# A cross-attention and spectral feed-forward kernel: Query fills ahead of the value products up to slot 12, GpSimd's long additions behind VectorE's zero test

## The chip, the cores and the metric

The kernel runs on one core of a Trainium2 chip. The metric is the device time of one execution in microseconds (us), the median of several runs. An execution is also recorded by the hardware profiler; its rows are what this document reads. Engines: PE is TensorE (PEld its weight loads), DVE is VectorE, ACT is ScalarE, POOL is GpSimd, SP is the queue that issues most DMAs.

## The reference

```python
x = x + xattn(layernorm(x), ctx, mask)      # 2 x 2048 tokens, 512 channels, 16 heads of 32, 128 keys
x = x + ffn(layernorm(x))

def xattn(z, ctx, mask):
    q, k, v = z @ wq + bq, ctx @ wk + bk, ctx @ wv + bv
    score = (q k^T / sqrt(32)) * mask
    score = where(score == 0, -1e9, score)
    return softmax(score) v @ wo + bo

def ffn(z):
    return real(ifft(fft(z) @ w_freq)) + bias
```

The feed-forward part is linear, so the kernel builds one real 512 x 512 matrix for it (fills U and M below) and multiplies by that.

## The kernel before, in words

The 4096 tokens are cut into 16 chunks of 256 (index `c`), the 16 heads into 4 groups of 4 (index `g`). One pair (chunk, group) is a step `s = 4c + g`; there are 64 steps. All engines run the same loop over slots `v` from 2 to 79, with `c, r = divmod(v, 4)`; each engine has its own fixed order inside a slot, and semaphores join them. There is no scheduler beyond `plan()` and the order in which each engine's code is written.

In slot v TensorE does, in this order (`plan()`, `items`):

1. PT(v-2): eight transposes of the exponentials of step v-2 (L540).
2. the slot's "mid" fills: WO (output projection, in slots with r = 0, 1), FF (feed-forward, r = 2, 3), and early in the program V, U and M.
3. S(v+1): the scores of the next step (L528).
4. PV(v-3): two transposes of the reciprocal sums (L553) and the products of step v-3 with the values (L557).
5. the slot's "late" fills: Query projections Q(c, f), twelve matmuls (L485) and one for the bias row (L488). Slots 2, 4 and 6 have two of them, the others one; from slot 55 there are none.

Fills go round three PSUM banks: `fill()` waits until VectorE has freed the bank of the fill three places before (`g_free`). In a slot with one mid fill a Query fill so waits for the mid fill of the slot before. Where fills come closer (the second Query fills of slots 4 and 6, the Query fills of slots 5, 7, 8 and 9, and the M fill of slot 11) the fill three places before is the Query fill before it.

ScalarE in slot v: `copy_rec(v-4)` (L655, waits for PV(v-4)), half of the exponentials of step v-1 (L642, wait for `nbias`), `copy_pt(v-2)` (L651, waits for PT(v-2)), the other half, `ctx_hi(v-4)` (L662, `ch`), in slots 9 to 12 `high_m` (L621, `mh`), then the high halves `qh` of the Query fills of the slot before (L616) and the `od` of U and M fills.

VectorE in slot v: `mask_mul(v)` (L799), `zero_to_neg(v)` (L806, the zero test: it writes `(z == 0) - z` over z), `ctx_norm(v-4)` (L822, `cn`), `least(v)` (L811), in slots 9 to 12 `low_m` (`ml`), then the low halves of the fills (L772 `ql`, which free the Query banks; L778, L784 for WO and FF), statistics, the reciprocal `rz` of step v-2 (L816), in slots 4 and 5 three additions `fold` (L854).

GpSimd in slot v: `spread(v-3)` (L1034, `rzb`, which PV(v-3) waits for), small statistics, `bias(v)` (L1028, `nbias`), subtractions for the feed-forward (L1003 `x1nl`), `add_bf`, `ctx_lo(v-4)` (L1039, `cl`, which WO waits for), `add_bo` (L990, adds the output bias to the input rows), `scale_mask` (L1021), `split_lo` (L983, `xtl`), and in slot 3 `low_o` (the low half `wol` of the output weights).

Of the kernel before, what the change touches and what calls it, by code (L numbers as in the profile page):

```python
# [5 lines left out]
ALU = mybir.AluOpType  # L6
# [6 lines left out]
D = 512  # L13
# [4 lines left out]
NC = NB * S // CH  # L18
NS = 4 * NC
V0, V1 = 2, NS + 16  # L20
LAST = ("FF", NC - 1, 1)
NEG = 1e9
MASK_SCALE = 1e-9 / 32.0 ** 0.5 / 8.0
# [2 lines left out]
NX = 7  # L26
NM = 4
NT = 2
# [6 lines left out]
def plan():  # L35

    fills, slots, held = [], {}, []
    lead = [("W1", 0), ("CT", 0), ("CT", 1), ("K", 0), ("ST", 0), ("Q", 0, 0), ("Q", 0, 1), ("S", 0),
            ("W1", 1), ("Q", 0, 2), ("S", 1), ("K", 1), ("Q", 0, 3), ("ST", 1), ("Q", 1, 0), ("S", 2),
            ("Q", 1, 1), ("Q", 1, 2), ("Q", 1, 3)]
    front = []
    for f in lead:
        if f[0] == "S":
            front += [("S", f[1], 0), ("S", f[1], 1)]
        else:
            front.append(("G", len(fills)))  # L50
            fills.append(f)
    early = {
        2: [("V", 0), ("ST", 2)], 3: [("V", 1)],
        4: [("U", 0)], 5: [("U", 1)], 6: [("U", 2)], 7: [("U", 3)],
        8: [("M", 0)], 9: [("M", 1)], 10: [("M", 2)], 11: [("M", 3)],
    }
    queries = {2: [(2, 0), (2, 1)], 3: [(2, 2)], 4: [(2, 3), (3, 0)], 5: [(3, 1)], 6: [(3, 2), (3, 3)]}
    for v in range(V0, V1):
        c, r = divmod(v, 4)
        mid = {  # L60
            0: [("WO", c - 2, 0)],
            1: [("WO", c - 2, 1)],
            2: [("FF", c - 3, 0)],
            3: [("FF", c - 3, 1)],
        }[r]
        mid = [f for f in mid if 0 <= f[1] < NC] + early.get(v, [])
        if mid == [LAST]:
            mid = [LAST, (*LAST, "right")]
        late = [("Q",) + f for f in queries.get(v, [divmod(v + 9, 4)]) if f[0] < NC]
        base = len(fills)  # L70
        fills += mid + late
        mids = list(range(base, base + len(mid)))
        lates = list(range(base + len(mid), len(fills)))
        items = []
        if 0 <= v - 2 < NS:
            items += [("PT", v - 2, 0), ("PT", v - 2, 1)]
        items += [("G", n) for n in mids]
        if 0 <= v + 1 < NS:
            items += [("S", v + 1, 0), ("S", v + 1, 1)]
        if 0 <= v - 3 < NS:  # L80
            items += [("PV", v - 3)]
        items += [("G", n) for n in lates]
        slots[v] = (items, held, mids)
        held = lates
    return fills, front, slots
# [6 lines left out]
def small_slot(c):  # L92
    return 2 if c == 3 else 4 * (c - 3)
# [4 lines left out]


def lo_slot(c):  # L100
    return 3 if c == 3 else 4 * (c - 3) + 2


def bo_slot(c):
    return c + 5 if c < 5 else 4 * (c - 3) + 3


def build(nc, x, xt, ctx_in, mask, wq, bq, wk, bk, wv, bv, wo, bo, lparts, tables, bf, eye, sums, pick, out):
# [3 lines left out]
    with ExitStack() as stack:  # L112
        def sem(name):
            return stack.enter_context(nc.semaphore(name))
# [6 lines left out]
        def sb(name, shape, dt, where=None):  # L121

            n = 2 if dt == F16 else 4
            for s in shape[1:]:
                n *= s
            n = (n + 31) // 32 * 32
            a = pos[0] if where is None else where
            if where is None:
                pos[0] += n
            assert a + n <= top, (name, a + n, top)  # L130
            return nc.alloc_sbuf_tensor_at(name, shape, dt, offset=a), a

        xs, _ = sb("xs", [128, NX, 2, D], F32)
        xtr, _ = sb("xtr", [128, NT, 4, CH], F32)
        xth, a_xth = sb("xth", [128, 2, 4, CH], F16)
        xtl, a_xtl = sb("xtl", [128, 2, 4, CH], F16)
# [35 lines left out]
        bob, _ = sb("bob", [128, D], F32)  # L172
# [41 lines left out]
        PB, CX, G = bank[0:2], bank[2], bank[3:6]  # L214
# [21 lines left out]
        g_free, tt_done, eq_done, mn_done = (sem(n) for n in ("g_free", "tt_done", "eq_done", "mn_done"))  # L236
# [5 lines left out]
        p_l1, p_l2, p_zero = (sem(n) for n in ("p_l1", "p_l2", "p_zero"))  # L242
        p_const, p_ms, p_nb, p_cl, p_st, p_xb, p_r2, p_x1b, p_sm, l_done, p_rz = (
            sem(n) for n in ("p_const", "p_ms", "p_nb", "p_cl", "p_st", "p_xb", "p_r2", "p_x1b", "p_sm", "l_done", "p_rz"))
# [6 lines left out]
        def tile_of(c, t):  # L251
            return 2 * c + t

        def columns(n):

            if fills[n] == LAST:
                return slice(0, 256)
            return slice(256, 512) if fills[n][:3] == LAST else slice(0, 512)

# [698 lines left out]
        def _(pool):  # L958
            small = [0]

            def step(ins):
                small[0] += 1
                ins.then_inc(p_sm, 1)
                pool.wait_ge(p_sm, small[0])
# [13 lines left out]
                step(pool.tensor_copy(z, h16[:].unsqueeze(2).broadcast_to([128, 2, 2, 2])))  # L978
                pool.tensor_tensor(stok[:, c % 2, :, 2:4], a, h16[:], ALU.subtract).then_inc(p_st, 1)

            def split_lo(c):
                pool.wait_ge(h1_done, c + 1)
                pool.tensor_tensor(xtl[:, c % 2], xtr[:, c % NT], xth[:, c % 2], ALU.subtract).then_inc(p_l1, 1)  # L983

            def add_bo(c, t):
                if c == 0 and t == 0:
                    pool.wait_ge(d_bb, 2 * 16)
                pool.wait_ge(a1_done, 2 * c + t + 1)
                z = xs[:, c % NX, t, :]
                pool.tensor_tensor(z, z, bob[:], ALU.add).then_inc(p_xb, 1)  # L990

            def rstd2(c, t):
                n = tile_of(c, t)
                pool.wait_ge(a2_done, n + 1)
                step(pool.tensor_scalar(ve2[:, t:t + 1], ag2[:, t, 1:2], EPS, SO * SO, ALU.add, ALU.mult))
                if n >= NO:
                    pool.wait_ge(g_free, at["FF", (n - NO) // 2, t] + 1)
                pool.tensor_tensor(rs2[:, n % NO:n % NO + 1], ve2[:, t:t + 1], half[:, 0, 0:1], ALU.pow).then_inc(p_r2, 1)
# [6 lines left out]
            def add_bf(c, t):  # L1005
                n = tile_of(c, t)
                pool.wait_ge(s2_done, n + 1)
                if c == NC - 1:
                    pool.wait_ge(l2_done, t + 1)
                else:  # L1010
                    pool.wait_ge(p_l2, n + 1)
                pool.wait_ge(p_r2, n + 1)
                z = x1[:, n % NO, :]
                pool.tensor_tensor(z, z, bfb[:], ALU.add).then_inc(p_x1b, 1)
# [15 lines left out]
            def spread(s):  # L1030
                pool.wait_ge(rz_done, s + 1)
                if s >= 2:
                    pool.wait_ge(pv_done, s - 1)
                pool.tensor_copy(rzb[:, s % 2], rz[:, s % 4, :].unsqueeze(2).broadcast_to([128, 8, 32])).then_inc(p_rz, 1)  # L1034
# [30 lines left out]
            def low_o():  # L1065
                pool.wait_ge(w_hi, 3)
                for i in range(2):
                    k = slice(2 * i, 2 * i + 2)
                    pool.tensor_tensor(wol[:, k], wos[:, k], woh[:, k], ALU.subtract).then_inc(o_lo, 1)
# [38 lines left out]
            for v in range(V0, V1):  # L1108
                c, r = divmod(v, 4)
                if v == 8:  # L1110
                    constant_row()
                if 0 <= v - 3 < NS:
                    spread(v - 3)
                for a in range(5, NC):
                    if small_slot(a) == v:
                        stat_cols(a)
                if r == 1 and 0 <= c - 2 < NC:
                    rstd2(c - 2, 0)
                if r == 2 and 0 <= c - 2 < NC:
                    rstd2(c - 2, 1)  # L1120
                if 0 <= v < NS:
                    bias(v)
                if r == 2 and 0 <= c - 2 < NC - 1:
                    norm_lo2(c - 2, 0)
                if r == 3 and 0 <= c - 2 < NC - 1:
                    norm_lo2(c - 2, 1)
                if r < 2 and 0 <= c - 3 < NC:
                    add_bf(c - 3, r)
                if 0 <= v - 4 < NS:
                    ctx_lo(v - 4)  # L1130
                for a in (3, 4):
                    if small_slot(a) == v:
                        stat_cols(a)
                for a in range(NC):
                    if bo_slot(a) == v:
                        add_bo(a, 0)
                    if bo_slot(a) + (2 if a >= 5 else 0) == v:
                        add_bo(a, 1)
                if r == 0 and 2 <= c + 1 < NC:
                    scale_mask(c + 1)  # L1140
                for a in range(3, NC):
                    if lo_slot(a) == v:
                        split_lo(a)
                if v == 3:
                    low_o()


def frequencies():
# [82 lines left out]
```

## Time and profile before

| | |
|---|---|
| median of 3 runs | 466.74 us (466.25 to 467.75) |
| profiled execution | 467.02 us |
| its span | 465.2 us |
| TensorE busy | 446.9 us, 96% |
| VectorE busy | 410.0 us, 88% |
| ScalarE busy | 375.9 us, 81% |
| GpSimd busy | 372.6 us, 80% |
| granted TensorE clock | 1.00 of full speed |

The span is the time between the first and the last recorded instruction; the profiled execution's own time is 1.8 us longer. A busy share is an average over the whole program: the start (to slot 12, about 120 us), the steady part and the end behave differently, and must be read apart. The first lines below name instructions by line of the kernel before.

### The profile page before, as it was taken

The numbers are of one execution on the slowest core, as the hardware profiler recorded it, in microseconds if no ns is written. First come the engines' busy times: TensorE is split into PE (matmuls) and PEld (weight loads), VectorE is DVE, ScalarE is ACT, GpSimd is POOL, SyncE is SP. The second block draws the span as 40 slices with busy tenths as digits, with TensorE's granted clock in tenths as the row PEclk, the third lists the DMA queues.
The fourth block names the chain that finished last, engine by engine and source line by source line (L and its number), as shares of the span: only waits on it lengthen the run. The fifth ranks groups of instructions, "written<-read, shape, count | busy, mean of one in ns | idle before, by whom it ended". The sixth has DMA issues, their size and how long they took to land.

```text
span 465.2 us, 11189 instructions
## 1 busy us (share of the span) xinstructions
PE 446.9 (96%) x3550; PEld 297.2 (64%) x3550; DVE 410.0 (88%) x627; ACT 375.9 (81%) x1432; POOL 372.6 (80%) x520
## 2 busy tenths in 40 slices
PE   7989977999999999999999999999999999999897
PEld 6777656676566666666666666666666666655444
DVE  3797499889999999999999999999999998999443
ACT  3359766789998989899989898998989898989720
POOL 6589666995989989898989898998989784876663
PEclk9999999999999999999999999999999999999999
DMA  8996644122435454545445454445342323340244
GB/s 290 394 360 171 235 173 113 45 82 70 104 76 138 115 138 105 141 120 132 131 116 134 104 130 117 107 108 144 103 103 57 99 75 77 82 92 20 73 103 124
DMA packets 83452, 59.36 MB, mean 128 GB/s; under 512 B 39746, under 2 KB 70978, under 8 KB 82883
## 3 DMA queue, kind: packets, MB, share of 16 engines
q1 hardware_dynamic: 82960, 58.55, 45.2%
q8 instruction: 29, 0.48, 0.4%
q14 instruction: 29, 0.23, 0.2%
q10 hardware_dynamic: 434, 0.10, 0.1%
HBM read 29.27 MB, written 8.39 MB: 81 GB/s over the span
## 4 chain that ended last, share of the span: by engine, by line
PE 79%; DVE 8%; issue 5%; POOL 4%; SPq 2%; DMA 1%; ACT 0%; POOLq 0%; DVEq 0%
PE bank L410 32%; PE bank L485 16%; PE bank L540 10%; PE bank L557 7%; PE scores L528 5%; PE bank L415 3%; PE bank L553 3%; DVE zs L799 2%; SPq L269 2%; PE bank L563 2%; DMA xs<-in_x 1%; DVE nmin L811 1%; PE bank L488 1%; DVE zs L806 1%; POOL cl L1039 1%
## 5 line engine op out<-in xcount | busy, mean ns | idle before, releaser
L642 ACT ACTIVATE zs<-zs,nbias 128x128 f32<-128x128 f32 x512 | 199.6, 397 | 6.4 <-POOL nbias L1028 6.2
L642 ACT ACTIVATION_READ_ACCUMULATOR zs<-zs,nbias 128x1 f32 x512 | 99.3, 194 | 0.0
L806 DVE SCALAR_TENSOR_TENSOR zs<-zs 128x1024 f32<-128x1024 f32 x64 | 94.8, 1481 | 2.2
L799 DVE TENSOR_TENSOR zs<-scores,ms 128x1024 f32<-128x1024 f32 x64 | 77.9, 1218 | 0.0
L811 DVE TENSOR_REDUCE nmin<-zs 128x8 f32<-128x1024 f32 x64 | 77.1, 1205 | 0.1
L651 ACT COPY pt<-bank 128x512 f32<-128x512 f32 x128 | 68.3, 586 | 7.0 <-PE bank L540 5.0
L485 PE MATMUL bank<-xth,wqh 128*128 128x256 f16 x256 | 70.3, 275 | 2.0 <-DVE kl L758 2.0
L485 PE MATMUL bank<-xtl,wqh 128*128 128x256 f16 x256 | 69.8, 273 | 0.0
L485 PE MATMUL bank<-xth,wql 128*128 128x256 f16 x256 | 69.8, 273 | 0.0
L540 PE MATMUL bank<-ident,zs 128*128 128x128 f32 x512 | 67.0, 274 | 0.5 <-ACT zs L642 0.5
L1034 POOL COPY rzb<-rz 128x256 f32<-128x256 f32 x64 | 61.0, 953 | 3.1 <-DVE rz L816 2.2
L540 PEld LDWEIGHTS bank<-ident,zs 128*128 128x128 f32 x512 | 56.8, 140 | 5.3 <-ACT zs L642 3.6
L1028 POOL TENSOR_SCALAR nbias<-nmin 128x8 f32<-128x8 f32 x64 | 15.7, 246 | 50.2 <-DVE nmin L811 50.2
L410 PE MATMUL bank<-woh,ch 128*128 128x512 f16 x128 | 48.5, 379 | 1.8 <-POOL cl L1039 1.8
L410 PE MATMUL bank<-woh,cl 128*128 128x512 f16 x128 | 48.5, 379 | 0.0
L410 PE MATMUL bank<-wol,ch 128*128 128x512 f16 x128 | 48.5, 379 | 0.0
L655 ACT COPY rec<-bank 128x256 f32<-128x256 f32 x64 | 23.9, 373 | 29.4 <-PE bank L557 29.0
L410 PE MATMUL bank<-mh,x1h 128*128 128x512 f16 x120 | 45.5, 379 | 0.0
L410 PE MATMUL bank<-mh,x1l 128*128 128x512 f16 x120 | 45.5, 379 | 0.0
L410 PE MATMUL bank<-ml,x1h 128*128 128x512 f16 x120 | 45.5, 379 | 0.0
L1039 POOL TENSOR_TENSOR cl<-cn,ch 128x256 f16<-128x256 f32 x64 | 43.5, 680 | 1.7 <-ACT ch L662 1.7
L528 PEld LDWEIGHTS scores<-ks,qs 96*128 96x128 f16 x480 | 31.8, 98 | 15.4 <-DVE zs L799 2.0
(109 smaller groups left out, 973.8 us busy)
## 6 DMA issues: line engine op xcount, KB each, us to landing
xs<-in_x SPq DMA_DIRECT2D x16, 512.0 KB, 4.2
xtr<-in_xt SPq DMA_DIRECT2D x16, 512.0 KB, 4.8
out<-x SPq DMA_DIRECT2D x31, 256.0 KB, 2.5
qs<-qh SPq DMA_DIRECT2D x120, 64.0 KB, 2.0
lp<-in_lparts SPq DMA_DIRECT2D x4, 1024.0 KB, 9.1
qs<-ql SPq DMA_DIRECT2D x60, 64.0 KB, 2.0
ms<-in_mask SPq DMA_DIRECT2D x16, 128.0 KB, 2.4
wqs<-in_wq SPq DMA_DIRECT2D x2, 512.0 KB, 6.7
```

What stands on the lines that cost most here:

```text
L410: last = pe.matmul(o, a, b, start=(i == 0), stop=(i == len(mm) - 1))
L485: pe.matmul(o[:, 0:256], a, b, start=(i == 0), stop=False)
L528: last = pe.matmul(A[:, n % 2, 128 * j:128 * j + 128], qs[c % 2][0:96, g, j, 128 * t:128 * t + 128], ks[0:96, g, j, c // (NC // NB), :], s ...
L540: last = pe.transpose(PB[f][:, a:a + 128], zs[:, s % NZ, t, 2 * f + i, :], ident[:])
L557: last = pe.matmul(CX[32 * j:32 * j + 32, 0:256], vs[:, b, h:h + 32], pt[:, s % 2, j, :], start=True, stop=True)
L642: last = act.activation(z, z, ACT.Exp, bias=nbias[:, s % 4, i:i + 1], scale=-NEG, accum_out=zsum[:, s % 4, i:i + 1])
L651: act.copy(pt[:, s % 2, 2 * f:2 * f + 2, :], PB[f][:]).then_inc(pt_copied, 1)
L799: dve.tensor_tensor(zs[:, s % NZ], A[:].rearrange("p t (h k) -> p t h k", h=4), ms[:, c % NM].unsqueeze(2).broadcast_to([128, 2, 4, KEYS]) ...
L806: dve.scalar_tensor_tensor(out=z, in0=z, scalar=0.0, in1=z, op0=ALU.is_equal, op1=ALU.subtract).then_inc(eq_done, 1)
L811: dve.tensor_reduce(nmin[:, s % 4, :], zs[:, s % NZ].rearrange("p t h k -> p (t h) k"), AX.X, ALU.min).then_inc(mn_done, 1)
L1034: pool.tensor_copy(rzb[:, s % 2], rz[:, s % 4, :].unsqueeze(2).broadcast_to([128, 8, 32])).then_inc(p_rz, 1)
L1039: pool.tensor_tensor(cl[:, c % 2, g, :], cn[:, s % 2, :], ch[:, c % 2, g, :], ALU.subtract).then_inc(p_cl, 1)
```

## The change

Three things are changed.

`plan()`: in slots up to 12 the late fills stand before PV(v-3). From slot 13 the order is as it was.

GpSimd, place and size of the two-tensor operations: `add_bo(a, 0)` and `split_lo(a)`, the latter cut into two halves in two slots, stand before `bias(v)` from slot 9 on, behind a new wait for `eq_done` (VectorE's zero test of this slot). `add_bo(a, 1)` is cut into halves three slots apart. The bias additions of chunks 0 to 2 go from slots 5, 6, 7 to slots 7, 8, 9, those of chunks 3 and 4 from 8, 9 to 11, 15 and those of later chunks from slot 4a-9 to 4a-1.

GpSimd, other moves: `spread(v-2)` at the end of slot v instead of `spread(v-3)` at the start, from slot 4 on; so it is ahead of `scale_mask` and `split_lo`. `low_o` in slot 3 goes ahead of `split_lo(3)`.

```diff
-        if 0 <= v - 3 < NS:
-            items += [("PV", v - 3)]
-        items += [("G", n) for n in lates]
+        weigh = [("PV", v - 3)] if 0 <= v - 3 < NS else []
+        queue = [("G", n) for n in lates]
+        items += queue + weigh if v <= 12 else weigh + queue
...
 def bo_slot(c):
-    return c + 5 if c < 5 else 4 * (c - 3) + 3
+    return c + 7 if c < 3 else 4 * c - 1
...
-                if 0 <= v - 3 < NS:
+                if v <= VP and 0 <= v - 3 < NS:      # VP = 4
                     spread(v - 3)
...
+                if VS <= v < NS:                     # VS = 9
+                    pool.wait_ge(eq_done, v + 1)
+                for a in range(5, NC):
+                    if v == 4 * a - 11:
+                        split_lo(a, slice(0, 2), False)
+                    if v == 4 * a - 10:
+                        split_lo(a, slice(2, 4))
+                for a in range(3, NC):
+                    if bo_slot(a) == v:
+                        add_bo(a, 0)
                 if 0 <= v < NS:
                     bias(v)
...
+                if v == 3:
+                    low_o()
                 if 0 <= v - 4 < NS:
                     ctx_lo(v - 4)
...
+                for a in range(3, NC):
+                    if bo_slot(a) == v:
+                        add_bo(a, 1, slice(0, D // 2), False)
+                    if bo_slot(a) + 3 == v:
+                        add_bo(a, 1, slice(D // 2, D))
+                for a in (3, 4):
+                    if lo_slot(a) == v:
+                        split_lo(a)
+                if v >= VP and 0 <= v - 2 < NS:
+                    spread(v - 2)
```

TensorE in slot 7, before: S(8), then PV(4), then Q(4, 0), then the first rows of slot 8 (the lines of the changed kernel are numbered three higher: 531 is 528, 488 is 485, 556 is 553).

```order
L528 MATMUL scores<-ks,qs_63 128x128 [waits d_q0,tt_done]
L528 MATMUL scores<-ks,qs_63 128x128 x3
L553 MATMUL bank<-ident,rzb 128x128 [waits p_rz,cn_done,pt_copied]
L553 MATMUL bank<-ident,rzb 128x128
L557 MATMUL bank<-pt,vs 32x256 x4
L485 MATMUL bank<-xth,wqh 128x256 [waits p_l1,w_lo,g_free]
L488 MATMUL bank<-srow,wz 128x256 [waits st_done,wz_lo]
L540 MATMUL bank<-ident,zs 128x128 [waits pt_copied,ex_done]
```

The same place in the changed kernel.

```order
L531 MATMUL scores<-ks,qs_63 128x128 [waits d_q0,tt_done]
L531 MATMUL scores<-ks,qs_63 128x128 x3
L488 MATMUL bank<-xth,wqh 128x256 [waits p_l1,w_lo,g_free]
L491 MATMUL bank<-srow,wz 128x256 [waits st_done,wz_lo]
L556 MATMUL bank<-ident,rzb 128x128 [waits p_rz,cn_done,pt_copied]
L556 MATMUL bank<-ident,rzb 128x128
L560 MATMUL bank<-pt,vs 32x256 x4
L543 MATMUL bank<-ident,zs 128x128 [waits pt_copied,ex_done]
```

The Query fill with its wait for a free bank now stands ahead of the products; of its thirteen matmuls the first and the last are shown, and of the scores the first half.

GpSimd in slots 4 and 5, before: `scale_mask(2)`, then slot 5 with `spread(2)`, `bias(5)`, `ctx_lo(1)`, both additions `add_bo(0)`, and `spread(3)`, which is slot 6's.

```order
L1021 TENSOR_SCALAR ms<-ms,rs_95 128x128 [waits p_st,d_m2]
L1021 TENSOR_SCALAR ms<-ms,rs_95 128x128
L1034 COPY rzb<-rz 128x256 [waits pv_done,rz_done]
L1028 TENSOR_SCALAR nbias<-nmin 128x8 [waits ex_done,mn_done]
L1039 TENSOR_TENSOR cl<-cn,ch 128x256 [waits ch_done]
L990 TENSOR_TENSOR xs<-xs,bob 128x512 [waits a1_done,d_bb]
L990 TENSOR_TENSOR xs<-xs,bob 128x512 [waits a1_done]
L1034 COPY rzb<-rz 128x256 [waits pv_done,rz_done]
```

The same stretch in the changed kernel.

```order
L1041 COPY rzb<-rz 128x256 [waits pv_done,rz_done]
L1028 TENSOR_SCALAR ms<-ms,rs_95 128x128 [waits p_st,d_m2]
L1028 TENSOR_SCALAR ms<-ms,rs_95 128x128
L1035 TENSOR_SCALAR nbias<-nmin 128x8 [waits ex_done,mn_done]
L1046 TENSOR_TENSOR cl<-cn,ch 128x256 [waits ch_done]
L1041 COPY rzb<-rz 128x256 [waits pv_done,rz_done]
```

`spread(2)` has gone ahead of the mask scaling, and the two additions have left slot 5.

GpSimd in slots 10 and 11 of the changed kernel: half of `split_lo(5)` and the addition `add_bo(3, 0)` stand ahead of the `nbias` of their slot, the first of them in a slot with the wait for `eq_done`.

```order
L986 TENSOR_TENSOR xtl<-xtr,xth 128x512 [waits h1_done,eq_done]
L1035 TENSOR_SCALAR nbias<-nmin 128x8 [waits ex_done,mn_done]
L1010 TENSOR_TENSOR x1nl<-x_76,x1nh 128x512 [waits h2_done]
L1046 TENSOR_TENSOR cl<-cn,ch 128x256 [waits ch_done]
L1041 COPY rzb<-rz 128x256 [waits pv_done,rz_done]
L995 TENSOR_TENSOR xs<-xs,bob 128x512 [waits a1_done,eq_done]
```

Before, both stood at the end of a slot, behind `ctx_lo`, and `split_lo` was one instruction of 1024 columns.

## Rows read from the trace of the kernel before

**Rows 1.** Busy time by stretch: start:end us, length, PE, PEld, DVE, ACT, POOL, clock, DMA.
```profile
57.60:117.00 59.40, 51.13 (x423) 38.76 (x422) 55.38 (x92) 46.96 (x183) 43.98 (x60) 1.00 0.33 97
120.00:390.00 270.00, 270.00 (x2228) 177.46 (x2229) 259.57 (x385) 244.08 (x948) 238.72 (x331) 1.00 0.44 113
390.00:436.00 46.00, 43.86 (x335) 24.84 (x334) 41.37 (x60) 43.87 (x184) 30.86 (x46) 1.00 0.31 72
```

**Rows 2.** Chain of waits, steady part: start us, us, what.
```profile
245.41 0.45 PE scores L528 x8
245.86 0.23 PE bank L553 x2
246.08 0.57 PE bank L557 x8
246.65 1.42 PE bank L485 x12
248.07 0.11 PE bank L488
...
251.64 0.45 PE scores L528 x8
```

**Rows 3.** Timeline of TensorE, start: start us, us, instruction [idle before <-releaser].
```profile
60.77 0.41 PE L553 MATMUL bank<-ident,rzb 128*128 128x128 f32 x2 [1.27 <-DVE cn L822]
...
69.22 0.41 PE L553 MATMUL bank<-ident,rzb 128*128 128x128 f32 x2 [1.47 <-POOL rzb L1034]
...
74.71 1.97 PE L415 MATMUL bank<-tb,lp 128*128 128x256 f32 x8 [2.11 <-issue]
...
85.45 0.41 PE L553 MATMUL bank<-ident,rzb 128*128 128x128 f32 x2 [0.93 <-POOL rzb L1034]
...
103.82 1.04 PE L540 MATMUL bank<-ident,zs 128*128 128x128 f32 x8
...
113.65 0.41 PE L553 MATMUL bank<-ident,rzb 128*128 128x128 f32 x2 [1.02 <-issue]
...
117.26 0.38 PE L410 MATMUL bank<-woh,ch 128*128 128x512 f16 x1 [0.24 <-POOL cl L1039]
```

**Rows 4.** Timeline of ScalarE in slots 8 and 9.
```profile
86.50 0.37 ACT L655 COPY rec<-bank 128x256 f32<-128x256 f32 x1 [0.58 <-PE bank L557]
...
91.23 0.37 ACT L616 CAST qh<-bank 128x256 f16<-128x256 f32 x1
...
99.19 0.63 ACT L621 ACTIVATE mh<-mf 128x512 f16<-128x512 f32 x1
```

**Rows 5.** Timeline of VectorE, slots 4 to 11.
```profile
57.60 1.22 DVE L799 TENSOR_TENSOR zs<-scores,ms 128x1024 f32<-128x1024 f32 x1
...
61.72 0.41 DVE L772 TENSOR_TENSOR ql<-bank,qh 128x256 f16<-128x256 f32 x1
...
63.52 1.99 DVE L854 TENSOR_TENSOR lp<-lp 128x512 f32<-128x512 f32 x3
...
70.74 3.87 DVE L854 TENSOR_TENSOR lp<-lp 128x512 f32<-128x512 f32 x3
...
91.66 0.41 DVE L772 TENSOR_TENSOR ql<-bank,qh 128x256 f16<-128x256 f32 x1
...
110.73 1.23 DVE L799 TENSOR_TENSOR zs<-scores,ms 128x1024 f32<-128x1024 f32 x1
```

**Rows 6.** Timeline of GpSimd, slots 5 and 6.
```profile
68.67 0.40 POOL L1034 COPY rzb<-rz 128x256 f32<-128x256 f32 x1
...
70.31 2.95 POOL L990 TENSOR_TENSOR xs<-xs,bob 128x512 f32<-128x512 f32 x2
...
81.84 3.13 POOL L983 TENSOR_TENSOR xtl<-xtr,xth 128x1024 f16<-128x1024 f32 x1
```

**Rows 7.** VectorE's zero test and least, all 64 each: ns min/median/max, first and last start.
```profile
L806 DVE SCALAR_TENSOR_TENSOR zs<-zs x64: 1224/1403/2486, 23.4 to 427.8; 128x1024 f32<-128x1024 f32 x64
```
```profile
L811 DVE TENSOR_REDUCE nmin<-zs x64: 1201/1203/1220, 25.0 to 429.4; 128x8 f32<-128x1024 f32 x64
```

## What I expect of the change

> **What bounds the kernel now.** I read the busy table by stretch first, then the chain of waits, then the timelines of the start. From 120 to 390 us TensorE is busy 270 of 270 us [rows 1], and the chain runs on TensorE alone: one slot takes 251.64 - 245.41 = 6.23 us, score to score [rows 2]. In it the Query fill costs 1.42 + 0.11 = 1.53 us, the products 0.23 + 0.57 = 0.80. Nothing that other engines gain there shortens the kernel. From 390 to 436 TensorE is busy 43.9 of 46 us and VectorE 41.4 [rows 1]; there are no Query fills left there. In the start, 57.6 to 117 us, TensorE has 59.4 - 51.1 = 8.3 us of idle time, VectorE 4.0 [rows 1]. The seven rows of its timeline show where: products that wait 1.27, 1.47, 0.93 and 1.02 us, a U fill that waits 2.11, a WO fill 0.24 [rows 3]. Only there can this change be worth anything: the order change ends at slot 12, and after it the program is TensorE's work, so a shift at slot 13 goes unchanged to the end.
>
> **GpSimd's moves, from slot 13 on.** They shorten VectorE's zero test, 1403 ns in the median and 1224 at least, up to 2486 [rows 7]. The gain per slot is 0.2 to 0.3 us of an engine that is busy 259.6 of 270 us but doesn't set the end: 0 us. The Trainium skill (SBUF — State Buffer, "SBUF: two separate sides") says that a VectorE instruction with two SBUF inputs and a GpSimd one that reads SBUF exclude each other for a whole instruction. The trace fits only in part: the 1024-column subtraction at 81.84 took 3.13 us beside a zero test. By that rule all 64 zero tests would fall to the least of them and VectorE would lose 64 x (1.48 - 1.22) = 16 us of work, and a kernel that VectorE bounds would gain as much; TensorE's full rows say that this one isn't.
> The new wait holds `nbias` and all behind it back. `least` takes 1.20 us in every one of 64 cases [rows 7], `cn` comes before it, so there are about 1.5 us for an addition of some 1.3 (I take half of the two in 2.95 less what the folds cost them, [rows 6]) or a half split of about 1.1. Cost 0; if it isn't covered, ScalarE's exponentials start late by up to 0.3 us once in four slots, which a slot's slack on ScalarE (270 - 244 over 43 slots, 0.6 us) takes in. In the end part nothing long is moved into VectorE's way: 0.
>
> **GpSimd's moves in the start.** The two additions that ran at 70.31 for 2.95 us leave slot 5. Beside them VectorE's three folds took 3.87 us, without them 1.99 [rows 5, 6]: VectorE gains 1.9 us just where the U fill waits 2.11 us for the folds [rows 3]. `spread(2)`, done at 68.67 behind the mask scaling, comes 1.7 us earlier, but see below. `low_o` before `split_lo(3)` takes about 0.2 us off the zero test of slot 4. On SP the load of chunk 5's transposed input waits for `split_lo(3)`, about 1 us later than before: it isn't needed for several slots. The DMAs that stack the Query of chunk 2 wait for the same `ql` as before, 0.2 us later: free.
>
> **The order change.** A Query fill ahead of the products fills the products' wait, but ScalarE's slot starts with a copy of the products' result. So the products 1.53 us later are ScalarE's whole slot 1.53 us later. That matters where the next Query fill waits for the bank of the one before: slots 4 to 9. The loop there is then: Query fill 1.53, products 0.80, to ScalarE 0.07 (85.45 + 0.41 + 0.57 against 86.50), from `rec` to `qh` 91.23 - 86.50 = 4.73, to `ql` 0.43, `ql` 0.41, back to TensorE 0.06: 8.03 us [rows 2 to 5]. Before, the products were not in this loop, and the copy with the first exponentials ran beside the Query fill. I walk through it, from slot 4, whose start at 57.60 hangs on a DMA and stays.
> - Slot 4: the second Query fill needs the `ql` of 61.72 + 0.41 [rows 5], now about 61.9. It runs 61.95 to 63.5, the products to 64.3. Before they ended at 60.77 + 0.98 = 61.75.
> - Slot 5: 64.3 + 0.07 + 4.73 + 0.43 + 0.41 + 0.06 = 70.0 for the Query fill; before it followed the products at 69.22 + 0.98 = 70.2. Gain 0.2; the filled wait of 1.47 us is worth no more, since the fill waits for its bank. Products end 72.3, before 70.2.
> - Slot 6: VectorE starts at 73.0 instead of 74.5 (1.9 less 0.4 of waiting for `qh`), the U fill at 73.2 instead of 74.7. But the second Query fill waits for the loop: 70.0 + 8.0 = 78.0. Products end 80.3. So the 1.5 us are given back.
> - Slot 7: loop 8.03 and one more ScalarE copy of about 0.26 (an estimate from its neighbours of the same size): 86.3. Before, 85.45 + 0.98 = 86.4. Even, but the products still have to come: transposes of slot 8 start 86.3 + 1.53 + 0.80 = 88.6, before 86.43 + 1.53 = 87.96: 0.7 late.
> - Slot 8: loop 94.3, TensorE's own work gives the same. Still 0.7.
> - Slot 9: loop with `mh` (0.53 on ScalarE, [rows 4]) and `ml` ahead of `ql`, about 0.3 net: 94.3 + 8.9 = 103.2. With products and the statistics row the transposes of slot 10 start at 105.6, before 103.9 [rows 3]: 1.7 late.
> - Slots 10 and 11: ScalarE has its copy at 105.7, `mh` ends 105.7 + 4.75 + 0.63 = 111.1; VectorE then has 2.4 us of `ml`, `ql`, M and statistics, so its slot 11 starts at 113.5 instead of 110.73 [rows 5]: 2.8 late. The products' wait at 113.65 (1.02) is covered, but the scores of step 12 now wait for VectorE, to 114.8.
> - Slot 12: WO waits for GpSimd's `cl`, which comes behind VectorE's slot 11: 113.5 + 3.9 for `nbias`, then 0.2 + 1.16 + 0.67 and the hand-over: 119.5, before 117.26 [rows 3]. With its 0.1 us of start-up saved: 2.1 late.
> - Slot 13: the products again come first and wait 0.5 us for a `cn` that is late: 2.6.
> Sum: 467.02 + 2.6 = 469.6 for an execution like the profiled one, which is 0.28 above the median: 469.3 us. Each of the five loops may be off by 0.15 us and the ends of slots 10 to 13 by 1: 468.1 to 471.0.
>
> **Rivals.** (A) Faster. ScalarE takes the later copy in (in slot 6 it idled before `ch`) and the fills wait for VectorE as before. Then the folds' 1.9 us and about 0.6 us of shorter zero tests stay, 2.5 us in all, and the products' waits no longer matter: 467.0 - 2.5 = 464.5, 464.2 against the median. For it: VectorE is busy 55.4 of 59.4 us in this stretch. Against it: the loop of 8.0 us is made of rows, and slots 5 to 7 already take 8 us each (69.22, 77.4, 85.45). It decides if `qh` comes in time for `ql` in slots 5 to 9. The skill's port rule is no more than a part of this case.
> (B) No change. The 0.7 us of slot 7 are kept, but slots 9 to 12 catch up because `mh` finds room: 467.4. For it: in slots 8 and 9 the loop and TensorE's work are equal to 0.1 us, so small errors decide whether lateness grows.
> (C) Slower still: in slots with r = 1 GpSimd reaches `nbias` late already, the half split adds 1.1 us before it, ScalarE's slack is not enough, and 0.3 us are lost in each of 13 chunks: 3.9 more, 473.2.
>
> **How the numbers follow.** The forecast has 0.60, A 0.18, B 0.17, C 0.05. A measurement can tell about 0.3%, 1.4 us, from no change: faster is under 465.3, slower over 468.1. B is within; of the forecast's 0.60 I count 0.04 as within. So faster 0.18, same 0.21, slower 0.61. The likeliest case's own range is 468.1 to 471.0. The range that is to hold 8 in 10 takes in B and the upper edge of A and leaves C out: 464.9 to 471.2.
>
> **What would show it.** Right: in slots 5 to 9 the Query fill waits for `ql` (1 to 3 us before it in slots 5 and 7), the products never wait, ScalarE's `rec` in slot 7 starts near 80.4 with no transposes to wait for; transposes of slot 8 near 88.6; WO of slot 12 near 119.5; slots after 13 still 6.23 us, zero tests from slot 9 on near 1.25 us. The three folds of slot 5 in 2.0 us. Wrong: if VectorE has no wait for `qh` in slots 6 to 8, it is A. If the steady slots are not 6.23 us, the argument that only the start counts falls.

## The result, and the profile after

| | before | changed kernel |
|---|---|---|
| median | 466.81 us (466.25 to 467.75, 4 runs) | 473.52 us (472.73 to 474.73, 4 runs) |
| profiled execution | 467.02 us | 474.20 us |
| span | 465.2 us | 472.4 us |
| granted clock, mean | 1.00 | 0.993 |

The ratio is 1.0139 (95% interval 1.0118 to 1.016): slower by 6.5 us (6.7 by the two medians), where 2.6 us were forecast. The direction was right, the time lies above the stated range of 464.9 to 471.2 us, and above the likeliest case's own, 468.1 to 471.0. It lies near the 473.2 us of rival C, but nothing of C's mechanism is seen below: that is chance.

Busy time of the changed kernel by the same stretches as [rows 1] (start:end us, length, PE, PEld, DVE, ACT, POOL, clock, DMA):

```profile
57.60:117.00 59.40, 50.87 (x385) 37.31 (x383) 47.23 (x81) 41.94 (x166) 34.05 (x53) 0.94 0.29 87
120.00:390.00 270.00, 268.46 (x2211) 175.92 (x2204) 248.41 (x391) 243.74 (x950) 232.77 (x353) 1.00 0.44 112
```

In the start TensorE has as much busy time as before for fewer matmuls (385 records against 423), and VectorE has 8 us less of it for fewer instructions (81 against 92): both get through less work in the same time. And the granted clock is 0.94 there, where it was 1.00.

The steady part is as it was, 250.85 - 244.62 = 6.23 us from score to score as in [rows 2], in the changed kernel's chain of waits:

```profile
244.62 0.45 PE scores L531 x8
...
250.85 0.45 PE scores L531 x8
```

The place where the time goes is TensorE's timeline of the start, which answers to [rows 3] (start us, us, instruction [idle before <-releaser]):

```profile
61.80 0.28 PE L488 MATMUL bank<-xth,wqh 128*128 128x256 f16 x1 [1.01 <-DVE ql L775]
...
69.74 0.28 PE L488 MATMUL bank<-xth,wqh 128*128 128x256 f16 x1 [2.36 <-DVE ql L775]
...
70.08 0.27 PE L488 MATMUL bank<-xth,wqh 128*128 128x256 f16 x1
...
71.14 0.42 PE L488 MATMUL bank<-xth,wqh 128*128 128x256 f16 x1
...
79.20 0.28 PE L488 MATMUL bank<-xth,wqh 128*128 128x256 f16 x1 [0.78 <-DVE ql L775]
...
87.41 0.40 PE L488 MATMUL bank<-xth,wqh 128*128 128x256 f16 x1 [2.63 <-DVE ql L775]
...
105.84 0.28 PE L488 MATMUL bank<-xth,wqh 128*128 128x256 f16 x1 [0.69 <-DVE ql L775]
...
117.44 0.62 PE L531 MATMUL scores<-ks,qs 96*128 96x128 f16 x8 [0.64 <-DVE zs L802]
...
122.83 0.38 PE L413 MATMUL bank<-woh,ch 128*128 128x512 f16 x1 [1.54 <-POOL cl L1046]
```

Up to slot 12 no products wait any more; five Query fills wait for `ql`, 7.5 us in all. And within the fill that starts at 69.74 the same matmul goes from 0.27 to 0.42 us: the clock has fallen. In the fill at 87.41 the first matmul already takes 0.40. The windows say so (start:end us, length, PE busy, granted clock, DMA):

```profile
66.00:69.00 3.00, 1.38 (x13) 1.00 0.00 0
69.00:72.00 3.00, 2.26 (x14) 0.72 0.18 43
72.00:75.00 3.00, 3.00 (x22) 0.71 0.41 97
...
84.00:87.00 3.00, 0.78 (x10) 1.00 0.00 0
87.00:90.00 3.00, 2.59 (x13) 0.56 0.18 44
```

Twice TensorE stands still for 2.4 and 2.6 us, and twice the clock drops from its upper level (2.4 GHz) to the lower one (1.2 GHz) for some 3.5 us behind that. Query fill and products, 2.33 us at full clock, took 73.69 - 69.74 = 3.95 and 91.36 - 87.41 = 3.95 us (both ends from the chain of waits): 1.6 us more, twice.

ScalarE in slot 7 shows the loop (timeline; the copy `rec` waits for the products, and all else follows it):

```profile
81.64 0.37 ACT L658 COPY rec<-bank 128x256 f32<-128x256 f32 x1 [2.69 <-PE bank L560]
...
83.47 1.05 ACT L654 COPY pt<-bank 128x512 f32<-128x512 f32 x2
...
86.25 0.37 ACT L587 CAST srow<-bank 64x256 f16<-64x256 f32 x1
86.52 0.64 ACT L619 CAST qh<-bank 128x256 f16<-128x256 f32 x2
```

VectorE waits 2.43 us for that `qh`, and TensorE at 87.41 for its `ql`.

What GpSimd's moves were to do, they do. The three folds of slot 5 take 2.17 us instead of 3.87, and the zero test 1225 ns in the median instead of 1403:

```profile
70.71 2.17 DVE L857 TENSOR_TENSOR lp<-lp 128x512 f32<-128x512 f32 x3
```
```profile
L809 DVE SCALAR_TENSOR_TENSOR zs<-zs x64: 1224/1225/1869, 23.5 to 434.9; 128x1024 f32<-128x1024 f32 x64
```

To follow the loss I compare the start of VectorE's `mask_mul(v)` in both traces, slot by slot: -0.1 us in slot 4, -1.7 in 6, +0.4 in 7, +1.5 in 8, +3.8 in 9, +4.7 in 10, +5.4 in 11, +5.6 in 12 and 13. From slot 43 to 60 it stays at +5.4 to +5.5. In slot 61 it jumps to +7.1, and so it ends. So two places: 5.5 us up to slot 13, 1.6 us in slot 60. The second I had not foreseen at all. GpSimd in slots 58 to 60 of the changed kernel:

```profile
412.31 0.68 POOL L1046 TENSOR_TENSOR cl<-cn,ch 128x256 f16<-128x256 f32 x1
412.94 1.71 POOL L995 TENSOR_TENSOR xs<-xs,bob 128x256 f32<-128x256 f32 x1
414.60 0.40 POOL L1041 COPY rzb<-rz 128x256 f32<-128x256 f32 x1
414.95 1.27 POOL L995 TENSOR_TENSOR xs<-xs,bob 128x512 f32<-128x512 f32 x1
416.20 0.23 POOL L1035 TENSOR_SCALAR nbias<-nmin 128x8 f32<-128x8 f32 x1
416.39 1.16 POOL L1010 TENSOR_TENSOR x1nl<-x,x1nh 128x512 f16<-128x512 f32 x1
417.52 1.65 POOL L1046 TENSOR_TENSOR cl<-cn,ch 128x256 f16<-128x256 f32 x1
```

and what TensorE waits for:

```profile
419.31 0.38 PE L413 MATMUL bank<-woh,ch 128*128 128x512 f16 x1 [2.17 <-POOL cl L1046]
```

The half addition `add_bo(14, 1)` of slot 58 begins beside a zero test and takes 1.71 us instead of some 0.7. The next addition, `add_bo(15, 0)`, so starts late, `nbias` comes some 0.7 us after the minimum that it needs (one slot earlier: some 0.2), and `cl` in its turn meets the next zero test (1.65 us instead of 0.68). The same WO fill waited 0.91 us before. In slots of 4.6 to 4.7 us, as slots 58 and 59 are, GpSimd has no time for this.

### The profile page after: what moved, and what is told of

It reads as the page before. It is cut to its first block, busy times and chain, and to the rows that moved or that the text cites. A ratio compares the mean times of both kernels' runs of the same rounds, so it can differ in the third digit from the quotient of the medians.

```text
span 472.4 us, 11248 instructions
## 1 busy us (share of the span) xinstructions
PE 449.0 (95%) x3550; PEld 297.9 (63%) x3550; DVE 395.1 (84%) x627; ACT 374.6 (79%) x1432; POOL 365.8 (77%) x544
## 4 chain that ended last, share of the span: by engine, by line
PE 74%; DVE 9%; issue 5%; ACT 4%; DMA 3%; POOL 2%; SPq 2%; POOLq 0%; DVEq 0%; ACTq 0%
PE bank L413 31%; PE bank L488 16%; PE bank L543 9%; PE bank L560 7%; PE scores L531 4%; ACT zs L645 3%; PE bank L556 3%; DVE zs L802 3%; SPq L272 2%; DMA cxs<-in_ctx 2%; DMA xs<-in_x 1%; PE bank L418 1%; PE bank L491 1%; DVE zs L809 1%; DVE nmin L814 1%
## 5 line engine op out<-in xcount | busy, mean ns | idle before, releaser
L809 DVE SCALAR_TENSOR_TENSOR zs<-zs 128x1024 f32<-128x1024 f32 x64 | 80.0, 1251 | 2.2
L488 PE MATMUL bank<-xtl,wqh 128*128 128x256 f16 x256 | 70.8, 277 | 0.0
L995 POOL TENSOR_TENSOR xs<-xs,bob 128x256 f32<-128x256 f32 (+1 forms) x45 | 45.5, 1013 | 21.0 <-DVE zs L809 21.0
L775 DVE TENSOR_TENSOR ql<-bank,qh 128x256 f16<-128x256 f32 x64 | 26.8, 423 | 33.3 <-ACT qh L619 33.3
L488 PEld LDWEIGHTS bank<-xth,wqh 128*128 128x128 f16 x256 | 25.2, 98 | 30.6 <-issue 13.2
```

The source lines that it names most:

```text
L488: pe.matmul(o[:, 0:256], a, b, start=(i == 0), stop=False)
L775: last = dve.tensor_tensor(ql[:, c % 2, f, :], src[:, 0:256], qh[:, c % 2, f, :], ALU.subtract)
L809: dve.scalar_tensor_tensor(out=z, in0=z, scalar=0.0, in1=z, op0=ALU.is_equal, op1=ALU.subtract).then_inc(eq_done, 1)
L995: i = pool.tensor_tensor(z, z, bob[:, n], ALU.add)
```

## Experiments

Theory 1: the Query fill ahead of the products lengthens a loop (products, ScalarE, `ql`, next Query fill), and TensorE's clock falls in its waits. Theory 2: GpSimd's moves and its new wait make the loss. The runs were taken in three sessions on three chips (the first four, the next four, the last two); each ratio is against the kernel before on the same chip in the same session, whose medians were 466.95, 467.05 and 466.99 us.

One thing has to be taken out before traces are compared. Slot 4 begins when VectorE gets a chunk's input rows, and they land at another time in each execution (VectorE's timeline; the kernel before, then the run of the order alone):

```profile
56.77 0.69 DVE L836 BATCH_NORM_STATS2 st<-xs 128x6 f32<-128x512 f32 x1 [3.76 <-DMA xs<-in_x]
```
```profile
55.72 0.69 DVE L836 BATCH_NORM_STATS2 st<-xs 128x6 f32<-128x512 f32 x1 [3.04 <-DMA xs<-in_x]
```

So a part of each shift at slot 13 is there at slot 4, before the changes act. It varies by more than 1 us even between kernels that are alike up to that slot. Counted from slot 4, the profiled runs agree to some 0.05 us where they should:

| shift of `mask_mul` against the kernel before, us | slot 4 | slot 13 | from 4 to 13 | falls of the clock between |
|---|---|---|---|---|
| changed kernel | -0.1 | +5.6 | +5.7 | 2 |
| order alone | -1.05 | +3.3 | +4.3 | 0 |
| GpSimd's moves alone | -0.8 | -2.9 | -2.0 | 0 |
| TensorE kept busy | -0.3 | +2.3 | +2.6 | 0 |
| end part mended | -0.6 | +3.6 | +4.2 | 1 |
| both remedies | +0.3 | +2.9 | +2.6 | 0 |
| copy behind the exponentials | -0.1 | -1.6 | -1.5 | 0 |
| best of both | -0.7 | -2.8 | -2.1 | 0 |
| three additions moved | +0.2 | +1.9 | +1.7 | 2 |
| order in slots 10 and 11 | -0.3 | -2.4 | -2.1 | 0 |
| best, copy late | -0.7 | -2.0 | -1.3 | 1 |

By this the start loses 2.6 us at full clock, which is what the forecast of 2.6 stands for: the order costs 4.3 by itself, and GpSimd's moves take back 1.7 of it. One fall of the clock adds 1.6, the two together 3.1.

**The order alone.** In the kernel before:

```diff
-        if 0 <= v - 3 < NS:
-            items += [("PV", v - 3)]
-        items += [("G", n) for n in lates]
+        weigh = [("PV", v - 3)] if 0 <= v - 3 < NS else []
+        queue = [("G", n) for n in lates]
+        items += queue + weigh if v <= 12 else weigh + queue
```

> The kernel before with only the order change of plan(): Query fills ahead of the products up to slot 12. Theory 1 (the loop from products over ScalarE to the next free Query bank, with TensorE's clock falling in its waits, makes the loss of the start): the shift at slot 13 is there again, +5 to +6.5 us, and the end part loses nothing: 472 to 473 us. Theory 2 (GpSimd's moves and their new wait make the loss): 466 to 468 us.

Measured: 472.01 us (470.28 to 473.18), ratio 1.0111 (1.0095 to 1.0127). The median is theory 1's. The five runs also tell what the clock does: 470.28 us at a mean granted clock of 1.000, 471.32 and 472.01 at 0.996, 472.76 and 473.18 at 0.993. In the profiled runs a mean of 0.996 goes with one fall and 0.993 with two. The profiled run is the first: 7.5 us of waits for `ql` in it, up to 2.6 us long, and yet no fall. There `mask_mul` of slot 13 is 3.3 us late, less than the 5 to 6.5 expected, and remains so to the end. So the clock fell in four of the five runs, not in all, and by these few runs each fall costs 1.0 to 1.7 us. Where it fell in the runs without a trace is not known.

**GpSimd's moves alone.** The changed kernel with the three lines of `plan()` put back.

> The changed kernel with the order of plan() put back as before: only GpSimd's moves. Theory 1: the start gains 1 to 2.5 us (the three folds of slot 5 in 2 us, no Query fill waiting 2 us for its bank, granted clock 1.00 in the start), the end part loses 1.6 us as in the changed kernel: 465.5 to 467.5 us. Theory 2: 471 to 473 us.

Measured: 467.39 us (465.75 to 469.85, 12 runs), ratio 1.0013 (0.9994 to 1.0032). Theory 2 is out. In the profiled run `mask_mul(13)` is 2.9 us earlier than before and that of slot 60 3.0 us; in slot 61 only 1.4 us are left. The runs fall into two groups: 465.75 to 466.80 us with a clock of 1.000 (six runs), 467.99 to 469.85 with 0.992 to 0.996 (six runs). Of the 2.9 us, 0.8 were there in slot 4, so the moves gain 2.0 us in the start. They lose 1.6 of it in slot 60, and in half of the runs the rest and more when the clock falls; the trace is of a run in which it didn't. Among the runs with a clock of 1.000 the mean is 466.28 us against 466.81 of the kernel before: 0.5 less, as 2.0 - 1.6 gives.

**TensorE kept busy in two waits.** In the changed kernel, called ahead of the Query fills of slots 5 and 7:

```diff
+            def keep(s):
+                pe.wait_ge(w_hi, 3)
+                pe.wait_ge(pt_copied, 2 * s + 2)
+                for i in range(16):
+                    pe.matmul(PB[0][:, 0:256], ident16[:], woh[:, 0, 0:256], start=True, stop=True)
```

> The changed kernel with 16 more matmuls (1.7 us, their result is never read) in each of the two waits of TensorE before the Query fills of slots 5 and 7. If the fall of the clock after these waits is on the path: granted clock 1.00 in 69 to 93 us, both Query fills in 1.5 us, 2.5 to 3.2 us less than the changed kernel, 470.3 to 471.0 us. If what the slow matmuls cost is hidden by ScalarE's loop: 473.5 us, no change.

Measured: 472.42 us (471.28 to 472.61), ratio 1.0108 (1.0094 to 1.0123). In the start it did what was expected: granted clock 1.00 in both places,

```profile
69.56 0.28 PE L488 MATMUL bank<-xth,wqh 128*128 128x256 f16 x1 [0.57 <-DVE ql L783]
...
85.71 0.28 PE L488 MATMUL bank<-xth,wqh 128*128 128x256 f16 x1 [0.84 <-DVE ql L783]
```

and `mask_mul(13)` is 2.3 us late instead of 5.6. Now the loop is seen without the clock, and from slot 4 on it costs what was forecast (2.6). The two falls cost 3.1 us. But the median came down by 1.1 us only and missed the expected range. In the profiled run the 2.2 us wait of slot 60 had a fall of the clock behind it:

```profile
416.02 0.38 PE L413 MATMUL bank<-woh,ch 128*128 128x512 f16 x1 [2.18 <-POOL cl L1054]
...
416.45 0.58 PE L413 MATMUL bank<-woh,cl 128*128 128x512 f16 x1
416.83 0.63 PE L413 MATMUL bank<-woh,ch 128*128 128x512 f16 x1
```

Slot 61 is 5.5 us late there, 3.3 more than slot 60: 1.6 for the wait and 1.7 for matmuls at half the clock. Two more of the four runs have the same mean clock of 0.996 and 472.3 to 472.5 us; the one at 1.000 took 471.28.

**The end part mended.** In the changed kernel:

```diff
-                for a in range(3, NC):
+                for a in range(3, NC - 2):
...
+                for a in (NC - 2, NC - 1):
+                    if bo_slot(a) - 8 == v:
+                        add_bo(a, 0)
+                    if bo_slot(a) - 6 == v:
+                        add_bo(a, 1)
```

The shorter range stands in both loops that call `add_bo`; chunks 14 and 15 are added 8 and 6 slots before `bo_slot`, in the new one.

> The changed kernel with the bias additions of the last two chunks done whole and eight to six slots earlier (slots 47, 49, 51, 53), behind ctx_lo, so that none stands in slots 55 to 62. If those additions make the loss of the end part (cl of slot 59 late, WO of slot 60 waits 2.2 us): 1.6 us less than the changed kernel, 471.9 us. If the end part is late for another reason: 473.5 us.

Measured: 471.34 us (469.66 to 473.20), ratio 1.0093 (1.0071 to 1.0114), 2.2 us less than the changed kernel. In the profile `mask_mul` is 3.4 us late in slot 54 and 3.6 in slot 63: the step in slot 60 is gone, and TensorE waits 1.03 us there instead of 2.17. The 0.6 us that were gained beyond the expectation would fit a fall of the clock behind that wait in some runs of the changed kernel, as the trace with TensorE kept busy has one. In the changed kernel's own trace there is none at that place, so this is not shown.

**Both remedies.** The additional matmuls and the end part mended.

> The changed kernel with both remedies: 16 matmuls that are never read in each wait of slots 5 and 7, and the bias additions of the last two chunks in slots 47 to 53. What is left is the loop over ScalarE alone, at full clock. If the terms add up (2.3 us at slot 13 in the run with the matmuls alone): 469 us, +2.2. If the clock falls elsewhere or the end part has another loss: 470.5 us or more.

Measured: 469.73 us (469.13 to 471.67), ratio 1.0057 (1.0036 to 1.0078); the clock is 1.000 in all six runs. `mask_mul` is 2.9 us late in slot 13 and 2.9 in slot 63. The terms add up: the start at full clock 2.6, clock in the start 3.1 when it falls twice, end part 1.6. That the matmuls hold the clock is borne out by the runs: without them, with the end part mended, the mean clock was below 1.000 in all six (0.999 in one). One run (471.67 us) is 1.7 us slower at a clock of 1.000, and why is open.

**ScalarE's copy behind the exponentials.** In the changed kernel with the end part mended:

```diff
-                if 0 <= v - 4 < NS:
-                    copy_rec(v - 4)
                 if 2 <= v - 1 < NS:
                     exps(v - 1, 0)
+                if 0 <= v - 4 < NS:
+                    copy_rec(v - 4)
```

> The changed kernel with the additions of the last two chunks in slots 47 to 53, and on ScalarE the copy of the products' result behind the first half of the exponentials instead of ahead of it. The order of plan() is the changed one. If the loss of the start comes from the products that ScalarE waits for at its slot's start: the loop loses 1.7 us or more, the waits for ql in slots 5 to 9 shrink, 464 to 467 us against 471.3 of the kernel with the additions alone mended. If the Query fills are late for another reason: 471 us.

Measured: 465.95 us (464.82 to 467.02), ratio 0.9972 (0.996 to 0.9983): 5.4 us less than the same kernel without this, which ran in another session. The order of TensorE is still the changed one. ScalarE in slot 7:

```profile
76.76 0.40 ACT L645 ACTIVATE zs<-zs,nbias 128x128 f32<-128x128 f32 x1 [0.50 <-POOL nbias L1035]
...
79.24 0.37 ACT L658 COPY rec<-bank 128x256 f32<-128x256 f32 x1 [0.83 <-PE bank L560]
79.79 1.07 ACT L654 COPY pt<-bank 128x512 f32<-128x512 f32 x2 [0.18 <-PE bank L543]
```

The exponentials no longer wait for the products, and the Query fill of this slot starts at 83.75 after a wait of 1.37 us. In the kernel with the end part mended alone, whose clock had not fallen up to there, it starts at 85.41 after 2.63. So it is ScalarE's place for this copy that ties the products to the Query banks: shown by breaking the tie. From slot 4 to 13 the loop's +2.6 us at full clock become -1.5, which is 4.1 of the 5.4 us; the rest fits the clock, which was 1.000 in eight of these eleven runs and in none of the other six. Even so the changed order gains nothing: GpSimd's moves with the order of before have -2.1 in the same place (next run).

**The best of both.** GpSimd's moves, the order of `plan()` as before, the end part mended.

> Both parts that the first runs blame taken out: the order of plan() as before, and the bias additions of the last two chunks in slots 47 to 53. The other moves on GpSimd stay. Theory (the loop over ScalarE, and the additions in the end part, are the whole loss; the rest of GpSimd's moves gains in the start): the 3.0 us gained at slot 13 in the run with GpSimd's moves alone reach the end, the 2.2 us wait of TensorE in slot 60 and the clock's fall behind it are gone: 463.5 to 464.5 us, with little spread. Rival (something else in the moves costs as much as they gain): 466 to 468 us.

Measured: 465.18 us (464.34 to 465.95), ratio 0.9957 (0.9943 to 0.997): faster than the kernel before by 1.9 us. The profile keeps its gain, 2.8 us in slots 13 and 63. The median gains less and is 0.7 us above the expectation, which fits the 3.0 us put in there: 0.8 of them were the earlier arrival in slot 4, not the moves'. Counted from slot 4 the moves gain 2.1 us, near what the median says. The mean clock is 1.000 in four and 0.996 in three of the seven runs.

**Three additions moved, nothing else.** In the kernel before:

```diff
-    return c + 5 if c < 5 else 4 * (c - 3) + 3
+    return c + 7 if c < 3 else c + 5 if c < 5 else 4 * (c - 3) + 3
```

> The kernel before with one move alone: the bias additions of chunks 0 to 2 in slots 7, 8, 9 instead of 5, 6, 7. If the gain of the start is the three folds of slot 5 that run 1.9 us shorter: 1.5 to 2 us, 465.0 to 465.5 us. If the earlier spread and the other moves make the gain: 466.9 us.

Measured: 468.58 us (467.83 to 471.78), ratio 1.0035 (1.0021 to 1.005): slower, a miss. The trace parts it in two. `mask_mul` is 1.1 us early in slots 6 to 8 and 1.5 in 9 and 10, 1.2 and 1.7 counted from slot 4. Then slot 9 of GpSimd's order has four additions, as I had left chunk 4 there, and `rzb` comes behind them (GpSimd's timeline, then TensorE's):

```profile
101.48 5.94 POOL L990 TENSOR_TENSOR xs<-xs,bob 128x512 f32<-128x512 f32 x4
107.36 0.86 POOL L1034 COPY rzb<-rz 128x256 f32<-128x256 f32 x1
```
```profile
108.37 0.47 PE L553 MATMUL bank<-ident,rzb 128*128 128x128 f32 x2 [2.82 <-POOL rzb L1034]
```

Slot 12 is 1.8 us late. This trace also has a fall of the clock in slot 4, at 61 us, and VectorE waits 0.56 us for `qh` behind it, which it doesn't in the best kernel. With as much added, an estimate, the folds are worth 1.2 + 0.6 = 1.8 us in slot 6, where GpSimd's moves together gain 2.0. So they are at least 1.2 us of it and may be nearly all; what the earlier `spread`, `low_o` and the shorter zero tests add is not shown.

**Two variants of the best.** The order change in slots 10 and 11 alone (`if v in (10, 11)` for `if v <= 12`), where a Query fill doesn't wait for the one before it:

> The kernel with GpSimd's moves and the end part mended (465.2 us), with the order change in slots 10 and 11 alone, where no Query fill waits for the bank of the one before it. The profile there shows the products of slot 11 waiting 1.02 us for cn and the scores 0.39. If the loop is what makes the order change bad, it is harmless here and fills that wait: 464.2 to 465.2 us. If later products hurt wherever they stand: 466 to 467 us.

Measured: 465.11 us (464.48 to 467.61), ratio 0.9964 (0.9949 to 0.998). Harmless where the bank is free, as the loop says, and of no use: the best kernel has 465.18, and from slot 4 to 13 both traces have -2.1 us. And ScalarE's late copy under the order of before:

> The same kernel (465.2 us) with the order of plan() as before everywhere, and on ScalarE the copy of the products' result behind the first half of the exponentials. Under the order of before the products are not in the loop of the Query banks, so this wait of ScalarE costs nothing: 465.2 us within 0.5. If ScalarE's wait for the products costs there too: 463.5 to 464.5 us.

Measured: 465.13 us (464.26 to 465.35), ratio 0.9949 (0.9934 to 0.9963): no difference to the best kernel either. Its trace has a fall of the clock in slot 4, which the best kernel's has not; VectorE then waits 0.66 us for `qh`, which would account for most of its -1.3 against -2.1. Outside the loop ScalarE's wait for the products is free, as far as the medians tell.

## Why the prediction was right about the loop and wrong in its size

- That only the start counts, and a shift at slot 13 goes unchanged to the end: the first half holds, the steady slots are 6.23 us. The second failed, below. The waits that the prediction lists are 7.0 of the 8.3 us of idle time; it left out one of 1.11 us at 58.88, where the scores of slot 4 wait for `zs`.
- The folds: forecast 1.9 us shorter, measured 1.7 (2.17 against 3.87). VectorE's slot 6 at 73.0 forecast, 72.8 measured; U's wait gone.
- The loop in slots 4 to 9: forecast Query fills at 61.95, 70.0, 78.0, 86.3 and 103.2. With the clock kept up they came at 61.62, 69.56, 77.50, 85.71 and 102.56, that is at a distance of 7.9, 7.9 and 8.2 us where 8.0, 8.0 and 8.3 were summed up. The loss at slot 13 was forecast as 2.6 and is 2.3 to 2.9 in two traces in which the clock holds, 2.6 in both when counted from slot 4. WO of slot 12 was forecast at 119.5 and came at 119.55 in the run with TensorE kept busy, whose slot 4 is 0.3 us early. Each loop came within 0.15 us of its forecast, so this part is right in its steps and not only in its sum.
- **The first mis-sized term is that the waits of 2 to 3 us before the Query fills of slots 5 and 7 were counted as waiting alone.** The prediction itself lists them (1 to 3 us before it in slots 5 and 7). It took the durations behind them from rows at full clock, and so put what follows a wait at nothing. In the profiled run TensorE's clock fell behind both, which cost 3.1 us. Where the order stood alone it fell in four runs of five.
- **The second is the step "In the end part nothing long is moved into VectorE's way: 0".** The end part has slots of 4.6 to 5.9 us instead of 6.23. The additions of chunks 14 and 15 now stand there (slots 55 to 62), and before there were none. The prediction looked at what GpSimd does to VectorE, not at what VectorE's zero test does to GpSimd's own line of work, which ends in `cl`. It cost 1.6 us, and where TensorE was kept busy in the start a fall of the clock on top.
- The new wait for `eq_done` and the halves before `nbias`: forecast free in the steady part; so it is. Rival C falls.
- Rival A was wrong about the order change but near about GpSimd's moves: alone they gain 2.0 us from slot 4 to 13, where it had 2.5. Rival B falls.
- The prediction says that the trace of before fits the exclusion of VectorE and GpSimd "only in part", because the subtraction at 81.84 took 3.13 us. It fits: the zero test had begun at 81.46 and ended at 82.9, and 2.13 us later, the usual time of this subtraction, it was done.
- Sum of what was found: 2.6 (the start at full clock, GpSimd's gain included) + up to 3.1 (clock in the start) + 1.6 (end part) = 7.3. The profiled run is 7.2 us late; in the medians it is 6.5 to 6.7, as two of the four runs have a mean clock of 0.996, one fall less.

## What to carry to other kernels

Filling a wait of the bounding engine with its next piece of work is worth nothing if that piece waits for a buffer which is freed by the chain behind the work now put last: write down the loop with both orders, and ask which instruction of a helping engine ties the two. Before a gain is read off two traces, look for the last place where both still do the same, and count from there: here up to 1.1 us of a shift was the arrival of a DMA. Where a change makes TensorE stand still for more than the profile of before shows, price the work behind the wait at the lower clock too, as a second case. And when work of a helping engine is spread evenly over the program, look at the part where the slots are shortest, because that is where it has no room.

## What the runs showed of the hardware that I had not expected

- TensorE's granted clock fell from 2.4 to 1.2 GHz behind standstills of 2.2 to 2.8 us, for some 3.5 us: at 69.74 and 87.41 in the changed kernel, at 416.02 with the matmuls added, at 108.37 in the kernel with three additions moved. It isn't certain: the run of the order alone had waits of 2.36 and 2.63 us and a clock of 1.000, and the kernel with the end part mended kept it behind 2.36 us and lost it behind 2.63.
- Nor does it take a wait of that length. In the kernel with three additions moved and in the last run it fell in slot 4 behind two waits of 1.27 and 1.10 us, and of 0.48 and 1.02 (TensorE's timeline of the last run; the third row takes 0.27 us at full clock):

```profile
58.16 0.62 PE L531 MATMUL scores<-ks,qs 96*128 96x128 f16 x8 [0.48 <-DVE zs L802]
59.80 0.41 PE L556 MATMUL bank<-ident,rzb 128*128 128x128 f32 x2 [1.02 <-issue]
...
61.08 0.42 PE L488 MATMUL bank<-xtl,wqh 128*128 128x256 f16 x1
```

  The kernel before has waits of 1.11 and 1.27 us there and kept its clock in the profiled run. But in other runs its clock fell too: the mean was below 1.000 in 12 of 17, 15 of 25 and 12 of 17 runs of the three sessions. That cost it little, 466.8 us on average at 1.000 and 467.5 at 0.993, so what a fall costs depends on where it comes. What decides whether it comes stays open.
- That makes runs of one kernel on one chip fall into groups: 465.8 to 466.8 us and 468.0 to 469.9 us for GpSimd's moves alone. With the clock held by matmuls that nobody reads, five of six runs lay within 0.9 us. A single profile of a kernel with such waits may show either.
- A GpSimd operation that begins while VectorE's zero test runs takes about 1 us longer (1.71 us for the addition of 256 columns instead of 0.73, 1.65 for a `cl` that takes 0.68 otherwise). The zero test itself loses little then. When GpSimd has begun first it is the other way round, as in the kernel before, where the subtraction takes its usual 2.1 us and the zero test twice its own 1.22 (GpSimd's timeline, then VectorE's):

```profile
360.24 2.14 POOL L983 TENSOR_TENSOR xtl<-xtr,xth 128x1024 f16<-128x1024 f32 x1
```
```profile
360.98 2.49 DVE L806 SCALAR_TENSOR_TENSOR zs<-zs 128x1024 f32<-128x1024 f32 x1
```

  So the wait for `eq_done` doesn't only spare VectorE: it also keeps GpSimd from beginning into a zero test. The half additions of `add_bo(a, 1)`, which stand behind `bias(v)`, have no such wait of their own.
